# From group 3 on, the first norm of an adaLN block acts on x laid out by channels, with deviation and shift as rows read back from HBM

## The reference

```
mod = silu(c) @ wmod            # 6 vectors of 128 channels per sample: sa, ca, ga, sb, cb, gb
h = layernorm(x) * (1 + ca) + sa
x = x + ga * attention(h)       # 8 heads, decayed linear-time attention, group norm, silu gate, Wo
h = layernorm(x) * (1 + cb) + sb
x = x + gb * ffn(h)             # token shift, sigmoid(r) * (relu(k)^2 @ Wv)
```

## Time and profile before

| | us |
|---|---|
| median of 3 runs | 752.81 (752.38 to 753.22) |
| the profiled execution | 752.51 |
| its span, first to last instruction | 750.7 |
| PE busy | 736.6 (98%) |
| DVE busy | 605.1 (81%) |
| POOL busy | 583.8 (78%) |
| ACT busy | 490.0 (65%) |

### The profile page before, as it was taken

One profiled execution on the slowest core, in us unless ns is written; L12 is line 12 of the kernel. 1 busy time (PEld: TensorE's weight loads), 2 busy tenths in 40 slices (PEclk: granted clock), 3 DMA queues, 4 the chain that ended last, 5 costly groups with the idle time before them and its releaser, 6 DMA issues.

```text
span 750.7 us, 29013 instructions
## 1 busy us (share of the span) xinstructions
PE 736.6 (98%) x12148; PEld 647.5 (86%) x12148; DVE 605.1 (81%) x1275; ACT 490.0 (65%) x953; POOL 583.8 (78%) x639
## 2 busy tenths in 40 slices
PE   6999999999999999999999999999999999999997
PEld 5778888888889889888888989888888988988886
DVE  6988687979888797987879788797987878787546
ACT  3576657566676766767666675756767566656665
POOL 2778788888789887898778888788878888787641
PEclk9999999999999999999999999999999999999999
DMA  9310000000111010011101011020111101001100
GB/s 325 107 38 17 17 17 13 19 17 16 23 31 35 12 45 17 24 37 29 28 13 46 18 27 31 10 52 16 25 29 31 31 16 30 17 9 31 24 15 29
DMA packets 56161, 25.67 MB, mean 34 GB/s; under 512 B 36184, under 2 KB 53856, under 8 KB 56032
## 3 DMA queue, kind: packets, MB, share of 16 engines
q1 hardware_dynamic: 55312, 23.02, 12.8%
q10 hardware_dynamic: 720, 0.80, 0.3%
HBM read 11.22 MB, written 4.20 MB: 21 GB/s over the span
## 4 chain that ended last, share of the span: by engine, by line
PE 94%; issue 2%; POOL 1%; ACT 1%; DVE 1%; DMA 0%; POOLq 0%; DVEq 0%
PE ring L306 53%; PE outs L306 15%; PE O_E L306 14%; PE ring L321 8%; PE O_O L306 3%; PE ring L351 2%; ACT y L744 0%; POOL qT L1308 0%; DMA X<-in_x 0%; POOL ln_rstd L1280 0%; POOL gn_rstd L1324 0%; ACT v L706 0%; ACT h2T L807 0%; DVE ln_stats L976 0%; DVE gn_sum L1052 0%
## 5 line engine op out<-in xcount | busy, mean ns | idle before, releaser
L1331 POOL TENSOR_TENSOR y<-y,gate 128x512 f32<-128x512 f32 x120 | 154.9, 1307 | 29.5 <-ACT y L744 29.5
L706 ACT ACTIVATE v<-ring 64x512 f32<-64x512 f32 x128 | 76.1, 595 | 81.4 <-PE ring L306 80.6
L1314 POOL TENSOR_TENSOR rot_k<-rot_k,sin_k 128x256 f32<-128x256 f32 x128 | 106.4, 852 | 24.4 <-DVE sin_k L1025 24.4
L306 PEld LDWEIGHTS outs<-wo_gated,y 128*128 128x128 f32 x992 | 119.7, 192 | 5.0 <-DVE y L1098 0.5
L306 PE MATMUL outs<-wo_gated,y 128*128 128x128 f32 x992 | 121.7, 275 | 0.1
L1052 DVE TENSOR_REDUCE gn_sum<-N 128x4 f32<-128x512 f32 x118 | 75.5, 681 | 42.4 <-ACT N L732 42.4
L1324 POOL TENSOR_TENSOR gn_rstd<-gn_var,minus_half 128x8 f32<-128x8 f32 x64 | 105.4, 1646 | 5.0
L1308 POOL TENSOR_TENSOR qT<-qT,swapped 128x512 f32<-128x512 f32 x64 | 82.9, 1295 | 28.3 <-DVE swapped L1008 27.8
L1032 DVE TENSOR_TENSOR A<-ring,consts 128x256 f32<-128x256 f32 x128 | 48.0, 415 | 59.9 <-PE ring L306 59.9
L744 ACT ACTIVATE y<-ring,gn 128x512 f32<-128x512 f32 x126 | 90.9, 776 | 5.2 <-PE ring L321 5.2
L714 ACT ACTIVATE kT<-ring 128x512 f32<-128x512 f32 x64 | 38.3, 598 | 77.5 <-PE ring L321 77.5
(11 more groups left out here) (172 smaller groups left out, 2090.5 us busy)
## 6 DMA issues: line engine op xcount, KB each, us to landing
k_odd<-rot_k SPq DMA_DIRECT2D x128, 64.0 KB, 2.3
X<-in_x SPq DMA_DIRECT2D x16, 256.0 KB, 4.0
out<-X SPq DMA_DIRECT2D x15, 256.0 KB, 2.5
key_tables<-in_const SPq DMA_DIRECT2D x7, 256.0 KB, 8.3
rotary_q<-in_const_q SPq DMA_DIRECT2D x2, 512.0 KB, 8.5
gates<-stored_rows SPq DMA_DIRECT2D x8, 128.0 KB, 3.2
N<-in_w_qkT SPq DMA_DIRECT2D x1, 512.0 KB, 5.1
N<-in_w_vT SPq DMA_DIRECT2D x1, 512.0 KB, 6.3
```

The lines of the kernel that those rows point to most:

```text
L306: return e.matmul(o, lhsT, rhs, start=start, stop=stop, skip_group_check=True)
L706: done = e.activation(v[halves(half), i % 2, 1, :, :], by(PAIRS, bank_of["v", odd, i][halves(1 - half), :]), ACT.Copy)
L1314: done = e.tensor_tensor(turned[:, n, :, :], turned[:, n, :, :], sin[:, n, :, :], op)
L1331: e.tensor_tensor(y[:, n % NY, :], y[:, n % NY, :], gate[:, n % 2, :], ALU.mult).then_inc(sem["y"])
```

## The change

The first norm of the groups 0 to 2 stays as it was. From group 3 on x is not turned on the chip any more: a second input `xT` holds x with channels on the partitions. The 1/deviation and the shift of the 512 tokens of a group lie with tokens on the partitions (`ln_rows`, 128 x 8); SP writes them to HBM as two rows of 512 (`written_rows`, one element of 4 bytes at a time) and reads both rows back onto all 128 partitions (`row_of`, 4 KB a partition, `spread_rows`). `load_turned` reads the group's part of `xT` (2 KB a partition). ACT multiplies the row of shifts by (1 + ca) and adds sa (`scale_rows`), DVE forms xT * (1 + ca) * deviation row (`apply_rows`), POOL adds the two (`add_rows`). Of the old chain `norm_apply`, `transpose_n` and `full_h` go. `norm_stats(g, 0)` and `norm_rstd(g, 0)` move one step ahead.

Two more things come with it: the tables of chunks 4 to 7 share one semaphore, and the scratch space for dynamic DMAs is 4096 (this makes room for the new tiles).

```diff
+BY_ROWS = 3
+EARLY_TABLES = 4
...
+        ln_rows = sb("ln_rows", [P, 2, 2, GC])
+        ln_rstd, ln_shift = ln_rows[:, :, 0, :], ln_rows[:, :, 1, :]
+        row_of = sb("row_of", [P, 2, W])
+        x_turned = sb("x_turned", [P, W])
...
+        written_rows = nc.dram_tensor("written_rows", (2, 2, W), F32, kind="Internal").ap()
...
+        def normed_by(g, which):
+            return ("rows_written", 16 * (g - BY_ROWS)) if which == 0 and g > BY_ROWS else ("ln_apply%d" % which, GC * g)
...
# PE
-                for g in due(step + 5, GC, NGROUP, 3):
-                    transpose_n(g, 0)
...
# ACT
+            def scale_rows(g):
+                b = g // GB
+                at.wait_ge("rows_read", 32 * (g - BY_ROWS + 1))
+                e.activation(row_of[:, 1, :], row_of[:, 1, :], ACT.Identity, bias=mod_cols[:, 0, b:b + 1],
+                             scale=mod_cols[:, 1, b:b + 1]).then_inc(sem["rows_scaled"])
...
-                for g in due(step + 7, GC, NGROUP, 3):
-                    norm_apply(g, 0)
+                for g in due(step + 8, GC, NGROUP, BY_ROWS):
+                    scale_rows(g)
                 for g in due(step - 8, GC, LAST):
                     norm_apply(g, 1)
...
# DVE
-                at.wait_ge(f"ln_apply{which}", GC * g)
+                at.wait_ge(*normed_by(g, which))
...
+            def apply_rows(g):
+                b = g // GB
+                at.wait_ge("rows_read", 32 * (g - BY_ROWS + 1))
+                at.wait_ge("hT_lo", g)
+                e.scalar_tensor_tensor(out=h_full[:, :], in0=x_turned[:, :], scalar=mod_cols[:, 1, b:b + 1], in1=row_of[:, 0, :],
+                                       op0=ALU.mult, op1=ALU.mult).then_inc(sem["rows_applied"])
...
-                for g in due(step + 8, GC, NGROUP, 4):
+                for g in due(step + 9, GC, NGROUP, 4):
                     norm_stats(g, 0)
...
-                for g in due(step + 5, GC, NGROUP, 3):
-                    full_h(g)
+                for g in due(step + 6, GC, NGROUP, BY_ROWS):
+                    apply_rows(g)
...
# POOL
+            def add_rows(g):
+                at.wait_ge("rows_applied", g - BY_ROWS + 1)
+                at.wait_ge("rows_scaled", g - BY_ROWS + 1)
+                e.tensor_tensor(h_full[:, :], h_full[:, :], row_of[:, 1, :], ALU.add).then_inc(sem["h_full"])
...
                 for g in due(step + 7, GC, NGROUP, 3):
                     low_h(g)
+                for g in due(step + 8, GC, NGROUP, BY_ROWS):
+                    add_rows(g)
...
-                for g in due(step + 11, GC, NGROUP, 4):
+                for g in due(step + 12, GC, NGROUP, 4):
                     norm_rstd(g, 0)
...
# SP
+            def load_turned(g):
+                at.wait_ge("rows_applied", g - BY_ROWS)
+                e.dma_start(x_turned[:, :], xT[:, g * W:(g + 1) * W]).then_inc(sem["rows_read"], 16)
+
+            def spread_rows(g):
+                at.wait_ge("ln_shift0", g + 1)
+                rows = written_rows[g % 2]
+                e.dma_start(rows.rearrange("k (j p) -> p (k j)", p=P), ln_rows[:, 0, :, :].rearrange("p k j -> p (k j)"), allow_slow_non_contiguous=True).then_inc(sem["rows_written"], 16)
+                at.wait_ge("rows_written", 16 * (g - BY_ROWS + 1))
+                at.wait_ge("h_full", g)
+                e.dma_start(row_of[:, :, :], rows.unsqueeze(0).broadcast_to([P, 2, W])).then_inc(sem["rows_read"], 16)
...
                 for i in due(step + 55, 1, NCHUNK, 4):
                     swap_k(i)
+                for g in due(step + 61, GC, NGROUP, BY_ROWS):
+                    spread_rows(g)
+                for g in due(step + 60, GC, NGROUP, BY_ROWS):
+                    load_turned(g)
...
-    nc = bacc.Bacc("TRN2", target_bir_lowering=False, num_devices=1)
+    nc = bacc.Bacc("TRN2", target_bir_lowering=False, num_devices=1, dynamic_dma_scratch_size=4096)
```

More of the change, by code:

```diff
@@ L51 @@
     "n_O", "o", "out0", "out1", "out2", "out3", "out4", "out5", "out6", "out_head", "product", "proj_k",
-    "proj_q", "proj_v_E", "proj_v_O", "qT", "r_psum", "r_tanh", "relu", "residual", "rot_k", "scaled", "scores",
+    "proj_q", "proj_v_E", "proj_v_O", "qT", "r_psum", "r_tanh", "relu", "residual", "rot_k", "rows_applied", "rows_read", "rows_scaled", "rows_written", "scaled", "scores",
     "silu_c", "sin_k", "sin_q", "small_consts", "sq_E", "sq_O", "state", "sum_E", "sum_O",
-    "swapped", "tables0", "tables1", "tables2", "tables3", "tables4", "tables5", "tables6", "tables7", "v_E",
+    "swapped", "tables0", "tables1", "tables2", "tables3", "late_tables", "v_E",
     "v_O", "v_mean", "v_sum", "w_ffn", "w_g", "w_g_hi", "w_g_lo", "w_k_hi", "w_k_lo",
@@ L85, in constants, with build @@
     return np.concatenate(parts, 1).astype(np.float32), rotary_q.astype(np.float32)
-def build(nc, x, cT, w_mod, w_qkT, w_gT, w_vT, w_oT, norm_wb, w_ffnT, ffn_mu, const, const_q, out):
+def build(nc, x, xT, cT, w_mod, w_qkT, w_gT, w_vT, w_oT, norm_wb, w_ffnT, ffn_mu, const, const_q, out):
     with ExitStack() as ctx:
@@ L257, in outs, with tables @@
             return [banks[j // PJ][:, j, :] for j in range(GC)]
+        def normed_by(g, which):
+            return ("rows_written", 16 * (g - BY_ROWS)) if which == 0 and g > BY_ROWS else ("ln_apply%d" % which, GC * g)
         def gates_of(b):
             return "gates%d" % (b % 2), 16 * (b // 2 + 1)
+        def tables(c):
+            return ("tables%d" % c, 16) if c < EARLY_TABLES else ("late_tables", 16 * (CB - EARLY_TABLES))
         def loaded(g):
@@ L687, in norm_apply @@
                 at.wait_ge(f"ln_shift{which}", g + 1)
-                at.wait_ge("n0T", min(g + NORM_AHEAD, NGROUP) if which else g)
+                at.wait_ge("n0T", min(g + NORM_AHEAD, BY_ROWS) if which else g)
                 at.wait_ge("n1T", g if which else g - NORM_AHEAD + 1)
@@ L779, in load_tables @@
                 columns = const[:, n_const + c * H * D:n_const + (c + 1) * H * D]
-                e.dma_start(key_tables[:, c, :, :, :].rearrange("p k h d -> p (k h d)"), columns).then_inc(sem["tables%d" % c], 16)
+                e.dma_start(key_tables[:, c, :, :, :].rearrange("p k h d -> p (k h d)"), columns).then_inc(sem[tables(c)[0]], 16)
             def last_apply(part):
                 at.wait_ge("last_shift", part + 1)
-                at.wait_ge("n0T", NGROUP)
+                at.wait_ge("n0T", BY_ROWS)
                 at.wait_ge("n1T", LAST)
@@ L1011, in rotate_k @@
                 c, bank = i % CB, bank_of["k", i]
-                at.wait_ge("tables%d" % c, 16)
+                at.wait_ge(*tables(c))
                 at.wait_ge("proj_k", i + 1)
@@ L1526 @@
         "x": lay(a(L0_attn_x)),
+        "xT": lay(a(L0_attn_x).reshape(B * T, C).T),
         "cT": lay(a(L0_c).T),
```

4 lines of the change are left out of this document (1 added, 3 removed).

## The result

975.62 us in the median (975.14 to 977.94) against 752.61 (752.38 to 753.22): ratio 1.297, interval 1.295 to 1.298. The profiled execution has a span of 974.2 us. I had forecast 948 (863 to 1005) and slower with 0.96, so sign, place and range held; the size was 27.6 us short.

What follows compares the result with a forecast made beforehand. PE, busy 98% of the span, was taken as the bound. 752.5 - 5.7 (transposes) + 92 (first wait) + 67 (second wait) + 42 (clock) = 948 us, range 863 to 1005.

Steps and rivals of the forecast that it cites:

- Transposes, -5.7: On PE, four transposes per group vanish, 0.44 us in each of 13 groups: -5.7 us.
- First wait: ACT's scale_rows waits for turned x in front of copy_kT, so PE's scores stand 7.2 us per group: +92 us.
- the point: On SP, the write's length from which it would delay the next k_odd pair: some 9.4 us; write expected 5.7.
- the rival of the slow write: On SP, the write exceeds 9.4 us, delaying k_odd and turned x; at 14 us, 60 more: 1008 us; chance 10%.
- the sign that I had named for it: On SP, a wait for the written rows beyond 9 us would show the forecast wrong.
- Second wait: DVE's earlier statistics wait for X in front of mask(4g-9); PE stands 7.5 us in 9 groups: +67 us.
- The 0.4 us for the banks of the state: On PE, after the second wait, a further wait for state banks that DVE frees later: 0.4 us.
- the rival of the clock: On PE, clock holds or costs little, part of slow work perhaps running beside late DVE: 906 us; chance 21%.
- Clock: TensorE's clock falls in each of 13 + 9 standstills and costs 1.9 us each: +42 us.
- Others at 0: Changed work on ACT, DVE and POOL, larger DMA traffic and the shared table semaphore: counted as 0.

Runs made afterwards that it cites:

- e13: Changed kernel with 32-byte write pieces read back strided, load_turned before the write, scale_rows one step later, statistics back in place, apply_rows moved: 747.76 us, ratio 0.9927.
- e11: Kernel before the change plus only the write of the rows in 4-byte pieces, which nobody waits for in time: 771.15 us, ratio 1.024.
- e12: Changed kernel with the rows written in 128 pieces of 32 bytes instead of 1024 of 4 (wrong results, timing only): 929.89 us, ratio 1.236.
- e10: e5 with the rows written in 128 pieces of 32 bytes instead of 1024 of 4 (wrong results, timing only): 759.77 us, ratio 1.009.
- e3: Changed kernel with load_turned issued in front of spread_rows in SP's list: 975.04 us, ratio 1.295.
- e2: Changed kernel with scale_rows one step later in ACT's list, behind copy_kT: 850.48 us, ratio 1.133.
- e7: Changed kernel with 38 dummy matmuls on PE in front of scores(4g-6), 13 times: 982.38 us, ratio 1.304.
- e8: Kernel before the change with only norm_stats(g, 0) and norm_rstd(g, 0) one step ahead, X's load unmoved: 819.41 us, ratio 1.088.
- e5: Changed kernel with X's load one step earlier on SP and scale_rows one step later on ACT: 797.13 us, ratio 1.057.
- e6: e5 plus the write of the rows one step earlier and load_turned in front of the read of the rows: 844.77 us, ratio 1.122.
- e4: Changed kernel with the write of the rows one step earlier and their read left in place: 1006.66 us, ratio 1.337.
- e1: Changed kernel with X's load one step earlier in SP's list: 930.18 us, ratio 1.236.

## Why the prediction held, and where it was short

**Transposes, -5.7: right.** e13 gains 4.9 of it once nothing else is in the way.

**First wait: the chain right, the size wrong.** I had 7.2 us per group, 92 in all; it was 10.0 and 129.6. The term that was mis-sized is the write. I extrapolated 5.7 us from the piece counts of k_odd and X, and set 9.4 us as the point from which it would matter. It kept SP waiting for 8.3 to 11.1 us. The point was wrong too: I read it from group 6 and wrote "the same in every group". In the odd groups the pair is due 2.7 us earlier, so there the point is some 6.7 us, and the write passed it in all seven; in the even groups it did so by little or not at all. That is the rival of the slow write, which had 10%, and the sign that I had named for it, a wait of SP beyond 9 us, came in eight groups. (The Trainium skill, DMA: Bandwidth & Descriptors, Specifications, says that transfers below 512 B are done as read-modify-write. I had set it aside because the 256-byte pieces of k_odd showed no price; at 4 bytes e11 and e12 show one, at 32 bytes e10 shows none like it. Whether read-modify-write is what costs it no run shows.) And I let the write cost nothing below the point, where it still cost 2.2 us, most of it because the late read of 512 KB travels with x_turned. Without the long write (e12) the wait is 6.3 us: from the 7.2, x_turned's landing after 2.9 instead of 3.5 takes 0.6, and the steps before and behind it another 0.3. So the place of x_turned makes 6.3 us of the wait if the write is short. In the changed kernel moving it alone gains nothing (e3), since the read of the rows is then as late.

**Second wait: right in its chain, too large.** DVE stood 7.3 us for X in group 6, as forecast (7). PE's wait for A was 5.6 there, 5.5 in the mean, not 7.5. From X's landing at 272.88 to v at 276.18 it took 3.3 us, where I had counted 4.1: the two mixing operations took 1.5 us together instead of 2.1. The 0.4 us for the banks of the state did not come; no wait of PE for S is in the list. And PE was due at v 5.0 us behind the end of sin_k (270.58 against 265.59), where I had 3.9 (221.06 against 217.2). 7.5 + 0.3 - 0.8 - 0.4 - 1.1 is the 5.5. The last of these terms is the overlap that the rival of the clock named, slow work of PE that runs beside DVE's wait. It is the smaller part: where no slow stretch comes before, the wait in group 6 is 5.9 us (e2) or 6.1 (e7), and 5.1 in the mean of e8, not 7.5.

**Clock: right.** 1.9 us was the forecast for each of 22; PE's extra busy time is 49.2 us, 2.2 each. In group 6 the stretch from scores(18) to outs took 9.01 instead of 7.06 us. That the clock falls inside a standstill, which no row of before could show, is now seen in both of group 6. The Trainium skill (TensorE: Matmul & The Clock Gate, section on the HAM clock gate) says that an idle array falls to its lower level, and the trace agrees; it came 2.1 us after PE's stop in the first standstill and some 5 us after it in the second, where it was back after 3.3 us instead of 10. The second cost less there, 1.4 us, but not everywhere: in group 7 the way from scores(23) to scores(24) took 18.86 us with 5.50 of waiting in it, against 10.91 before with 0.44 for the transposes, so 2.9 were lost.

**Others at 0: wrong by one.** Missing was a cost of the write to those who don't wait for it, 1.4 us each time alone (e11). The changed kernel shows no such gap (PE's idle time with "issue" is 0.6 us in all), probably because PE stands there anyway; it came out only when the waits were gone (e5, e6), and ruled in e4.

The errors were +37.6 us on the first wait, -17.4 on the second and +7.2 on the clock: 27.4 of the 27.6 between forecast and result. That the result lay so near is partly luck: the first standstill (129.6; its own range was 79 to 101) and the second (49.6; 61 to 80) both left their ranges, in opposite directions.

## What to carry to other kernels

When a DMA enters a schedule, ask for its place in the issuing engine's list first and its size second: here a 256 KB read behind the wrong pair cost 6 us per group and a 4 KB write 4, and mending one of the two alone gained nothing for the read (e3) and 46 us for the write (e12). Read the room at that place in more than one period: here the two pairs of k_odd are 11.9 us apart in one group and 9.2 in the next. A write in 4-byte pieces is better sent in the order in which it lies, and turned by the access pattern of the reader, even if the reading operations take a quarter to two thirds longer. The prices of two standstills in one period are not independent, and adding them needs a check: taking away the second made the first longer (e1), and filling the first lengthened both (e7).

## What the runs showed of the hardware that I had not expected

- 1024 pieces of 4 bytes to HBM: packets through the DMA engines within 2 us, end seen after 8 to 14 us (9.0 to 12.5 in the changed kernel); 128 pieces of 32 bytes of the same 4 KB: landed after 1.7 to 3.4 us (e10, e12).
- Behind such a write some 16 KB packets of instructions took 3.4 to 4.2 us (seven in e11) instead of 0.96, others their usual time, and PE stood for up to 1.9 us with "issue" (e11). With a store queued behind it, that store took 14.7 us instead of 2.7 (e4).
- Standstills of like length don't cost alike. Behind 5.6 us of idling PE was slow for 3 us (changed kernel, group 6), behind 6.1 us for 6 (e7); the clock had fallen 5 and 2 us after the stop. And a shorter one need not cost less: 6.3 us of standing (e12) cost as much as 10.0.
